# Attention in one fused kernel: the output product of a unit from bf16 high and low parts

## The reference

```python
q = _rope(split_heads(_conv(_mcl(x, Wq, bq), q_conv_w, q_conv_b, 3)))
k = _rope(split_heads(_conv(_mcl(x, Wk, bk), k_conv_w, k_conv_b, 3)))
v = split_heads(_conv(_mcl(x, Wv, bv), v_conv_w, v_conv_b, 3))
qk = jnp.einsum('bceqd,bcekd->bceqk', q, k) / math.sqrt(h)     # 8 heads of 32
a = jax.nn.softmax(qk, axis=-1)                                # 512 x 512 per head
o = jnp.einsum('bceqk,bcekd->bceqd', a, v)
return _conv(_mcl(o, Wo, bo), o_conv_w, o_conv_b, 0)           # _mcl: F x F per channel
...
x = x + _L0_conv_ref(_gn(x), ...)
x = x + _L1_conv_ref(_gn(x), ...)
```

## Time and profile before

| | us |
|---|---|
| median of three runs | 1193.09 |
| lowest, highest | 1192.31, 1193.65 |
| the profiled execution | 1192.17 |
| its span | 1190.4 |
| TensorE busy | 1064.7 (89%) |
| VectorE busy | 818.7 (69%) |
| GpSimd busy | 767.5 (64%) |
| ScalarE busy | 712.0 (60%) |
| the tail products, L1159 | 70.0 |

### The profile page before, as it was taken

The page is one execution under the profiler, slowest core; times in us unless marked ns, Lnnn a source line. Parts: engine busy times, 40 slices in busy tenths (PEclk is TensorE's granted clock), DMA queues, the critical chain, the costliest instruction groups (busy, mean ns, idle before and its releaser), DMA issues. The chain is left out here.

```text
span 1190.4 us, 25545 instructions
## 1 busy us (share of the span) xinstructions
PE 1064.7 (89%) x10352; PEld 565.2 (47%) x10352; DVE 818.7 (69%) x1174; ACT 712.0 (60%) x1164; POOL 767.5 (64%) x782
## 2 busy tenths in 40 slices
PE   0899999999998989999888988999976789899997
PEld 0777777777761233333333333333322345454553
DVE  5888665555569978888888888888831974444344
ACT  3877767777653666666667666666674332346345
POOL 1144455555453988999988888999994019909900
PEclk9999999999995999999999999999998899899999
DMA  9944433433356764462717344551000999765761
GB/s 304 305 131 121 124 94 108 138 100 100 90 149 152 123 155 69 81 105 58 114 38 121 76 84 78 90 98 37 19 18 28 323 346 287 237 232 160 199 205 47
DMA packets 137765, 159.05 MB, mean 134 GB/s; under 512 B 17856, under 2 KB 85712, under 8 KB 137644
## 3 DMA queue, kind: packets, MB, share of 16 engines
q1 hardware_dynamic: 114544, 122.58, 42.1%
q10 hardware_dynamic: 14560, 25.66, 6.3%
q0 software_dynamic: 8544, 9.18, 2.9%
HBM read 106.54 MB, written 52.89 MB: 134 GB/s over the span
## 5 line engine op out<-in xcount | busy, mean ns | idle before, releaser
L1264 POOL TENSOR_TENSOR a_pl<-a_prob 128x512 bf16<-128x512 f32 x416 | 442.6, 1093 | 37.5 <-ACT a_prob L1217 37.0
L1217 ACT ACTIVATE a_prob<-a_col 128x512 f32<-128x512 f32 x512 | 288.7, 596 | 150.1 <-PE a_col L1122 143.3
L1170 DVE TENSOR_REDUCE a_negmax<-a_row 128x1 f32<-128x512 f32 x384 | 246.4, 681 | 55.3 <-PE a_row L1101 54.4
L501 PE MATMUL f_acc<-f_wh,f_xhl 128*32 128x384 bf16 x2560 | 163.5, 327 | 0.0
L619 DVE TENSOR_TENSOR f_yl<-f_acc,f_yh 128x768 bf16<-128x768 f32 x80 | 76.3, 956 | 88.5 <-ACT f_yh L727 88.5
L1181 DVE TENSOR_TENSOR a_pl<-a_prob 128x512 bf16<-128x512 f32 x96 | 115.8, 1207 | 20.6 <-ACT a_prob L1217 20.6
L850 POOL TENSOR_TENSOR f_straight<-f_straight,f_turned 128x832 f32<-128x832 f32 x40 | 85.5, 2137 | 65.6 <-DVE f_turned L645 65.6
L1122 PE MATMUL a_col<-a_q,a_k 98*128 98x512 bf16 x256 | 97.8, 389 | 30.7 <-ACT a_prob L1217 26.9
L1122 PE MATMUL a_col<-q,k 98*128 98x512 bf16 x256 | 100.0, 391 | 22.3 <-ACT a_prob L1217 20.7
L1528 PE MATMUL b_acc_s<-b_xh,b_mat_h 128*104 128x512 bf16 x256 | 99.4, 388 | 10.3 <-DVE b_xl L1618 9.3
L501 PE MATMUL f_acc<-f_wl,f_xhl 128*32 128x384 bf16 x1280 | 107.7, 326 | 0.0
(11 more groups left out here) (174 smaller groups left out, 2093.2 us busy)
## 6 DMA issues: line engine op xcount, KB each, us to landing
X<-b_x ACTq DMA_DIRECT2D x16, 526.0 KB, 8.4
a_v<-V SPq DMA_DIRECT2D x16, 512.0 KB, 4.7
Z<-a_z ACTq DMA_DIRECT2D x32, 256.0 KB, 2.0
b_z<-Z SPq DMA_DIRECT2D x16, 512.0 KB, 10.7
b_x<-in_x SPq DMA_DIRECT2D x32, 256.0 KB, 10.0
b_res<-X SPq DMA_DIRECT2D x38, 208.0 KB
out<-b_y ACTq DMA_DIRECT2D x38, 208.0 KB
V<-f_vout SPq DMA_DIRECT2D x64, 104.0 KB
```

Of the source, the lines that this page charges most:

```text
L501: last = nc.tensor.matmul(acc[half][c * KW:(c + 1) * KW, part, 0:PART], xx[g % 2][:, (half * QUAD + c) * FH + f, at], ww[half * QUAD + c][ ...
L1170: nc.vector.reduce_max(negmax[n % PAIR][:, 0, t:t + 1], row[step % ROWS][:], AX.X, negate=True).then_inc(max_done, 1)
L1217: nc.scalar.activation(prob[sets_done % RING][:, t % QUAD, :], col[step % 2][:], ACT.Exp).then_inc(exp_done, 1)
L1264: nc.gpsimd.tensor_tensor(pl[p][:, r, :], prob[p][:, r, :], ph[p][:, r, :], ALU.subtract).then_inc(lo_pool, 1)
```

## The change

The tail product is made from bf16 parts. High parts are not computed: `oh` and `wh` are the upper halves of the fp32 words of `oT` and `wo`, read as bf16 with a step of two. Low parts are made by GpSimd into new tiles `ol` (one per half of a unit) and `wl` (one per load of the weights, so in units 0, 1, 4, 5, 8, 9, 12 and 13). Each fp32 matmul becomes three bf16 ones: high by high, low weight by high head, high weight by low head. The tail waits for the low parts; the whole tail and the copies behind it are moved back by one slot.

```diff
+        oh = [t[:].bitcast(BF16).rearrange("p f (w t) -> p f w t", t=2)[:, :, :, 1] for t in oT]
+        ol = [sb(f"a_ol{s}", [P, FH, W], BF16) for s in range(2)]
+        wh = [t[:].bitcast(BF16).rearrange("p f (n t) -> p f n t", t=2)[:, :, :, 1] for t in wo]
+        wl = [sb(f"a_wl{s}", [P, FH, F], BF16) for s in range(CHANNELS)]
...
-        TAIL = KEEP + QUAD * QT + 3
+        TAIL = KEEP + QUAD * QT + 4
...
-                        pe.wait_ge(divided, SETS // QT * (n + 1))
+                        pe.wait_ge(o_low, FH * (n + 1))
                         pe.wait_ge(max_kept, min(n + 2, UNITS))
-                        pe.wait_ge(wo_in[n % CHANNELS], 32 * (n // PAIR + 1))
+                        pe.wait_ge(w_low, n // PAIR * CHANNELS + n % CHANNELS + 1)
...
+                cols = slice(j * P, (j + 1) * P)
                 for f in range(FH):
-                    last = nc.tensor.matmul(out[:, at], wo[n % CHANNELS][:, f, j * P:(j + 1) * P], oT[n % 2][:, f, at], start=f == 0, stop=f == FH - 1)
+                    for r, (ww, oo) in enumerate(((wh, oh), (wl, oh), (wh, ol))):
+                        last = nc.tensor.matmul(out[:, at], ww[n % CHANNELS][:, f, cols], oo[n % 2][:, f, at],
+                                                start=f == r == 0, stop=f == FH - 1 and r == 2)
...
+                act.wait_ge(wo_in[n % CHANNELS], 32 * (n // PAIR + 1))
                 nc.scalar.activation(z[j][:], out[:], ACT.Identity, bias=bo[n % CHANNELS][:, j:j + 1]).then_inc(out_kept, 1)
...
-            pipeline(units(EXP - 1, v_low) + lows(EXP + 1, low_part, True))
+            def output_low(n, m):
+                pool.wait_ge(divided, SETS // QT * n + m + 1)
+                if m == 0 and n >= 2:
+                    pool.wait_ge(out_full, FH * (n - 1))
+                nc.gpsimd.tensor_tensor(ol[n % 2][:, m, :], oT[n % 2][:, m, :], oh[n % 2][:, m, :], ALU.subtract).then_inc(o_low, 1)
+
+            def weight_low(n):
+                if n // CHANNELS % B == 0:
+                    c = n % CHANNELS
+                    pool.wait_ge(wo_in[c], 32 * (n // PAIR + 1))
+                    if n >= PAIR:
+                        pool.wait_ge(out_full, FH * (n - CHANNELS * (B - 1) + 1))
+                    nc.gpsimd.tensor_tensor(wl[c][:], wo[c][:], wh[c][:], ALU.subtract).then_inc(w_low, 1)
+
+            pipeline(units(EXP - 1, v_low) + lows(EXP + 1, low_part, True) + quads(KEEP + 1, output_low) + units(KEEP + QUAD, weight_low))
```

More of the change, by code:

```diff
@@ L956, in attend @@
         divided = sem("a_divided")
+        o_low = sem("a_o_low")
+        w_low = sem("a_w_low")
         out_full = sem("a_out_full")
```

## The result

The changed kernel takes **1233.82 us** (median of 5 runs, 1227.84 to 1236.44) against **1192.31 us** for the kernel before in runs of the same series (5 runs, 1190.20 to 1193.65). The ratio is **1.0352, 95% interval 1.0329 to 1.0375**: 3.5% slower. The forecast was 1229, range 1211 to 1243. The profiled execution took 1227.84 us, its span is 1226.0 (before: 1190.4), its mean granted clock 0.964 (before: 0.978).

The account below looks back on a forecast made before the run. A TensorE-ScalarE ping-pong set the 33.20 us period, GpSimd close behind; after the change, a TensorE-GpSimd loop. Loops and ends +25.4 us, clock +10.9, together +36.3 on the 1193.09 median: 1229 us, range 1211 to 1243.

Parts of the forecast that it names:

- The mechanism: Attention stage: TensorE's tail waits for GpSimd, GpSimd for the division; loops of 34.5 or 35.5 us against 33.20.
- the first tail: First unit: its tail was forecast to start at 423.65, against 420.28 before the change.
- the fifteenth loop: Last loop before the fifteenth tail: 33.1 us, without row scores and with a shorter low part of v.
- Products: Tail: six bf16 matmuls take 0.66 us a part instead of 0.87, so 0.84 us less a unit.
- Rival E: Tail products: loads of strided weights aren't hidden, 38 us more, 1256 to 1267; chance 0.05.
- GpSimd's new work: GpSimd: two head low parts a unit, a weight one in 8 units, 1.03 us each, 2.6 a unit in the mean.
- GpSimd's wait for the division: GpSimd before the first half's head low part: stands still about 2 us once per unit.
- Copy of the first output half: Tail: ScalarE makes this copy one slot later, behind an exponential not hidden by a mix set; 0.77 us more a unit.
- The clock: TensorE behind the eight 2.8 us tail waits: lower granted clock costs 1.36 us each, +10.9 us.
- Rival A: TensorE behind the tail waits: the clock stays up, 1218.5 us; chance 0.25.
- The last unit and the end: From the fifteenth tail on: +0.15 for GpSimd's low parts, +1.1 for a head low part, -1.3 for cheaper last products.
- Rivals C and D: GpSimd: new work fits idle time, C 1179.5 us, chance 0.03; D no change, 1190 to 1197, chance 0.07.

Follow-up runs that it names:

- The filled wait: Changed kernel plus eight useless bf16 products on TensorE before the tail's wait for the low parts: 1222.75 us, ratio 1.0257 against the kernel before.
- The split: Changed kernel with second half's low part on VectorE, first half's eight slots later on GpSimd, tail one slot earlier: 1188.66 us, ratio 0.9969 against the kernel before.
- the products alone: Changed kernel with all three products on high parts, no new low parts on GpSimd, tail slot kept: 1182.61 us, ratio 0.9914 against the kernel before.

## Why the prediction was right

**The mechanism** is the one named: a loop between the two engines, through the division and the low parts. The waits of the tail are 1.9 and 2.9 us (1.8 and 2.8 forecast), the loops at full clock 34.62 and 35.62 (34.5 and 35.5), and the first tail is at 423.47 (423.65). The runs that take links away confirm it: without the low parts, or with one of them on VectorE and the other far from its division, the loss is gone. One thing was put too simply. I treated the division's wait as what ties the engines together. The run with the first half's low part moved removed it, and lost only 0.07 us of a loop without a weight low part; the exponentials behind the tail close the loop as well.

**The terms.** The fifteenth tail was forecast 25.46 us later, plus 10.9 for the clock: 36.4. It is 40.21 later, 3.85 more. Of these, 13 loops are 0.12 us longer (1.6), the fifteenth loop is 35.18 - 1.60 = 33.58 instead of 33.1 (0.5; the slow stretch from 909 to 918 lies in it, so that may be the clock's too), the first tail is 0.2 sooner, and the clock makes 1.9.

- *Products:* 0.21 us saved a part forecast, 0.19 measured; with everything else as before 0.81 us a unit for 0.84. Rival E (strided weights at 0.21 us a product) is out: 0.11.
- *GpSimd's new work:* 1.03 forecast, 1.03 to 1.04 measured for a head or weight low part.
- *GpSimd's wait for the division:* some 2 us forecast, 1.23 measured. What is missing went into waits for exponentials (0.49 and 0.52) and into the three low parts behind it, 3.48 us instead of 3.04. The low part of v got shorter in return, 2.13 us for 2.53 in the earlier trace rows. The sum held because such shifts cancelled, not because each term was right.
- *Copy of the first output half:* 0.77 forecast, 0.61 measured.
- *The clock:* eight falls forecast at 1.36 us; eight measured at 1.60, so 12.8 for 10.9. The price was taken from the one fall in the earlier trace rows, behind a wait for a DMA, where the work differs. Which waits bring a fall was right only in number: one of the long ones didn't, one of the short ones did. The filled wait shows the term: no fall is left behind a tail, and the fifteenth tail comes 11.9 us sooner. Between the spans it is 9.7, since the last loop is 2 us longer there. Rival A (clock stays up) had 1218.5; the filled run, with eight products more in each tail, has 1222.75.
- *The last unit and the end:* -0.1 us forecast from the fifteenth tail on, -0.2 measured up to the last stage (40.21 to 40.0).

That the spans differ by 35.6 us, close to the +36.3 of the forecast, is luck: the attention stage lost 40.0 us for 36.3, and a last stage that was 4.4 us shorter, with no edit in it, hid the difference. Between the medians it is 41.5 us. The forecast had the mechanism right and the time some 5 us too short.

**Rivals C and D** (GpSimd's new work fits into its idle time) fell. Its idle time is real, and lies where it can't be used. That the place in the order matters, with the same amount, is shown by the first half's low part moved on GpSimd, 13.2 us less on the same chip. The split is 45.2 us away, but it changes three things at once, and one low part a unit leaves GpSimd; the tail's slot alone is worth 3.5 us with the products alone and 6 with both low parts on VectorE. The amount is not nothing either: in the loop read above GpSimd works 32.4 of 34.62 us, so with all the work on it and no idle time the period would be about the old 33.20. No run kept all of it on GpSimd and lost nothing.

**What stays open.** The last stage took 258.6 us in the profiled execution of the changed kernel and 263.0 in that of before, and 257.7 to 264.1 in the eleven other runs, with no edit in it. The change moves the medians by 41.5 us and the profiled spans by 35.6; that difference is of this size. Why the stage varies I have not settled, nor why the clock fell behind some 1.9 us waits and not behind others, nor what brings the slow stretches in the last two units.

## What to carry to other kernels

Busy sums don't tell whether an engine has room: ask where in the period its idle time lies, and which engine waits for the instruction that is put behind its backlog. Work that sits between two steps of a loop belongs on the engine that made its input, or far enough from the step that needs it. A stop of 2 to 3 us in front of dense matmuls can cost 1.6 us beyond its length, since what follows may run at the lower clock; and before work is moved to VectorE, price its two-input instructions beside GpSimd's and not alone.

## What the runs showed of the hardware

- Waits of 1.9 us in front of the tail were enough to bring TensorE to the lower clock behind some of them (five tails of the kernel without weight low parts), at 1.60 us each. Eight products of 512 columns in the wait, with 1.09 us of it left idle, kept the clock at 1.00 from 417 to 900.
- Beside fp32 products, behind the same waits, the clock fell behind eleven tails of thirteen instead of seven, and four of these slow stretches cost 3.0 us instead of 1.6.
- bf16 products whose both operands are every second 16-bit word of an fp32 tile start 0.11 us apart for 256 columns, as dense ones do; in the run of the products alone six of them take 0.69 us (457.86 to the next product at 458.55).
- VectorE's low part of 128 x 512 took 0.69 us with GpSimd at rest, 1.59 and once 2.62 beside it, and 1206 to 1374 ns in the mean. GpSimd's own, 1.01 to 1.08 as a rule, took 1.49 at 549.61 in the split, where VectorE had begun one at 549.44 (0.76 us).
